# An audio tower on one core: first weight's transfer issued by ScalarE, VectorE's thresholds and floors moved, fewer spare products, a first expert unit in one piece

## The reference

```
h = patches @ W.T + b                                 # embedding
# block 0: attention with quantised activations and ternary weights
xq = act_quant(layernorm(h))                          # x * 127/max|x|, rounded, back
q, k, v = act_quant(heads(bit_linear(xq, W)))         # for Wq, Wk, Wv
   # bit_linear: s = clip(mean(|W|), EPS); Wq = clip(round(W / s), -1, 1) * s
w = act_quant(softmax(q k' / sqrt(32)));  y = act_quant(w v)
h = h + act_quant(bit_linear(y, Wp))
# 16 experts, the best two of a token weighted by a softmax
scores = x @ router_w ; g = x @ gate_w[e] ; u = x @ up_w[e]
h = h + sum_e combine[e] * ((silu(g) * u) @ down_w[e])
# block 1: attention over 4 positions, then a gated FFN between two Hadamard transforms
```

## Time and profile before

| | |
|---|---|
| median of 3 runs | 281.83 us (281.79 to 283.18) |
| profiled execution | 282.39 us, its span 280.6 us |
| TensorE busy | 264.8 us, 94% |
| VectorE busy | 227.1 us, 81% |
| ScalarE busy | 149.4 us, 53% |
| all transfers | 40.43 MB |

### The profile page before, as it was taken

One profiled execution on the slowest core, in us unless ns is written; L12 is line 12 of the kernel. 1 busy time (PEld: TensorE's weight loads), 2 busy tenths in 40 slices (PEclk: granted clock), 3 DMA queues, 4 the chain that ended last, 5 costly groups with the idle time before them and its releaser, 6 DMA issues. The chain is left out here.

```text
span 280.6 us, 3960 instructions
## 1 busy us (share of the span) xinstructions
PE 264.8 (94%) x1477; PEld 217.6 (78%) x1480; DVE 227.1 (81%) x409; ACT 149.4 (53%) x234; POOL 6.3 (2%) x19
## 2 busy tenths in 40 slices
PE   8779789989999999999999999999999999999993
PEld 3445454658899999989999897766689989999872
DVE  1969999897999988889898676888958894878783
ACT  2798772345563565655555524535466662653530
POOL 0200000000000000000000000000100000000000
PEclk9999999999999999999999999999999999999998
DMA  6960899904244808172630068095000000000003
GB/s 229 427 250 2 290 378 411 446 12 139 86 159 181 306 33 336 23 316 74 262 110 6 0 224 374 2 363 238 0 0 2 0 2 0 0 2 0 2 2 75
DMA packets 6997, 40.43 MB, mean 144 GB/s; under 512 B 1217, under 2 KB 1473, under 8 KB 5314
## 3 DMA queue, kind: packets, MB, share of 16 engines
q1 hardware_dynamic: 6978, 40.18, 37.6%
HBM read 39.13 MB, written 0.52 MB: 141 GB/s over the span
## 5 line engine op out<-in xcount | busy, mean ns | idle before, releaser
L1101 PE MATMUL bank<-s_xf_hi,s_f_hi 128*128 128x256 f32 x128 | 31.2, 282 | 0.5 <-ACT s_xf_hi L675 0.5
L1101 PE MATMUL bank<-s_xf_hi,s_f_lo 128*128 128x256 f32 x128 | 31.1, 281 | 0.0
L543 ACT ACTIVATE s_silu<-bank 128x192 f32<-128x192 f32 x32 | 10.5, 331 | 36.6 <-PE bank L883 32.6
L883 PE MATMUL bank<-s_w_hi,s_xt_hi 128*128 128x384 f32 (+1 forms) x128 | 29.3, 350 | 0.6 <-DVE s_h L1417 0.6
L883 PE MATMUL bank<-s_w_lo,s_xt_hi 128*128 128x384 f32 (+1 forms) x128 | 27.9, 339 | 0.3 <-DVE s_w_lo L1431 0.3
L883 PE MATMUL bank<-s_w_hi,s_xt_lo 128*128 128x384 f32 (+1 forms) x128 | 27.7, 338 | 0.3 <-DVE s_xt_lo L1194 0.3
L1101 PEld LDWEIGHTS bank<-s_xf_hi,s_f_hi 128*128 128x128 f32 x128 | 24.1, 188 | 1.1 <-issue 0.7
L1625 DVE TENSOR_TENSOR s_f_lo<-s_ffn_raw,s_f_hi 128x1024 fp32r<-128x1024 f32 x16 | 19.6, 1225 | 6.0 <-ACT s_f_hi L622 5.9
L1101 PEld LDWEIGHTS bank<-s_xf_hi,s_f_lo 128*128 128x128 f32 x128 | 24.1, 188 | 0.4
L883 PEld LDWEIGHTS bank<-s_w_hi,s_xt_hi 128*128 128x128 f32 x128 | 21.9, 188 | 2.2 <-DVE s_h L1417 0.8
L883 PEld LDWEIGHTS bank<-s_w_lo,s_xt_hi 128*128 128x128 f32 x128 | 22.8, 188 | 0.7 <-DVE s_w_lo L1431 0.7
(11 more groups left out here) (235 smaller groups left out, 559.7 us busy)
## 6 DMA issues: line engine op xcount, KB each, us to landing
s_moe_raw<-moe_gu SPq DMA_DIRECT2D x16, 768.0 KB, 7.2
s_ffn_raw<-ffn_w SPq DMA_DIRECT2D x4, 2048.0 KB, 10.9
s_moe_raw<-moe_dn SPq DMA_DIRECT2D x8, 768.0 KB, 4.4
s_big_raw<-att_w SPq DMA_DIRECT2D x4, 1024.0 KB, 8.9
s_big_raw<-down_w SPq DMA_DIRECT2D x4, 1024.0 KB, 8.0
s_l_raw<-l_w SPq DMA_DIRECT2D x1, 2560.0 KB, 21.1
out<-s_h SPq DMA_DIRECT2D x4, 128.0 KB, 2.3
s_tok_w<-tok_w SPq DMA_DIRECT2D x1, 256.0 KB, 2.6
```

The costliest lines, as they stand in the source:

```text
L543: act.activation(B["silu"][i % 2][:], unit_bank(i)[:, 0:F], ACT.Silu).then_inc(silu_done, 1)
L883: ins = pe.matmul(unit_bank(i)[:, 0:n], xt(k, t)[part % 2], w[:, k, 0:n], start=(first and k == 0), stop=(last and k == KC - 1))
L1101: pe.matmul(tb(j, n)[:, 0:TOK], M[w][j][:, k, n * P:(n + 1) * P], M["xf_hi"][:, k, :], start=(w == "w_hi" and k == 0), stop=False)
```

## The change

It has four parts: ScalarE and no longer SyncE issues the transfer of `att_w[0]`; in the projections' stretch the small VectorE steps stand elsewhere, the query's score factor is computed by ScalarE, and the spare products between projections are gone (12 instead of 18 before the value sums); the low part of expert 0's rest is computed while tile 0 is mixed, and that of expert 1's main part before tile 1's low input; unit 0 is computed in one piece, and unit 2 is split around unit 1.

```
-        WARM, GAP, FILL = (18, 24), 20, 7
+        WARM, GAP, FILL = (12, 24), 20, 7
 @block.sync
-            for m in range(4):
+            for m in range(1, 4):
                 if m == 2:
                     sp.dma_start(con[:], consts[:, 0:K_REP]).then_inc(ld_con, 16)
                 sp.dma_start(big_raw[:, m * KC * C:(m + 1) * KC * C], att_w[m]).then_inc(ld_att[m], 16)
 @block.scalar
+            act.dma_start(big_raw[:, 0:KC * C], att_w[0]).then_inc(ld_att[0], 16)
             act.wait_ge(bias_done, 1)
...
             main_high(1)
+            act.wait_ge(g_ready, 1)
+            act.activation(A["sh"][:, 5], A["g3"][:, 0], ACT.Copy, scale=float(D) ** -0.5).then_inc(gx_ready, 1)
             act.wait_ge(g_ready, 3)
 @block.tensor
             project(0, 0, 1)
+            weight_total(2, bank[3][:, 0:1])
             project(0, 1, 1)
-            weight_total(2, bank[3][:, 0:1])
-            early_warm(6, bank[1])
             for n in range(2):
                 for t in range(TILES):
                     project(1, n, t)
-                early_warm(6, bank[1])
             pe.wait_ge(half_ready, 3)
             for n in range(2):
                 for t in range(TILES):
                     project(2, n, t)
-                early_warm(6, bank[1])
...
+            pe.wait_ge(gu_ready, 1)
             unit_products(0, 0, True, False)
-            keep_warm(bank[5], 4)
+            unit_products(0, 2, False, False)
             pe.wait_ge(xt_ready, 3)
-            unit_products(0, 1, False, False)
+            unit_products(0, 1, False, True)
             pe.wait_ge(su_ready, 1)
             transposes(3, B["xn"], 1)
-            pe.wait_ge(gu_ready, 1)
-            unit_products(0, 2, False, True)
+            pe.wait_ge(guh_ready, 2)
+            pe.wait_ge(resth_ready, 2)
+            pe.wait_ge(turned, TURNS_FIRST)
+            unit_products(2, 0, True, False)
             pe.wait_ge(xt_hi_ready, 4)
             unit_products(1, 0, True, False)
             unit_products(1, 2, False, False)
             pe.wait_ge(xt_ready, 4)
             unit_products(1, 1, False, True)
-            pe.wait_ge(turned, TURNS_FIRST)
-            unit(2)
+            unit_products(2, 1, False, False)
+            pe.wait_ge(gu_ready, 2)
+            unit_products(2, 2, False, True)
             unit(3)
 @block.vector
+            floors(0)
             transposed_out(1)
             largest(0, 0)
-            floors(0)
+            floors(1)
+            weight_scale(2, bank[3][:, 0:1])
             largest(0, 1)
             head_factors(0)
             head_round(0, q16_ready)
-            weight_scale(2, bank[3][:, 0:1])
             head_steps(0)
-            floors(1)
             floors(2)
-            dve.wait_ge(g_ready, 1)
-            o.mark(dve.tensor_scalar(sh[:, 5], g3[:, 0], float(D) ** -0.5, None, ALU.mult))
...
-            weight_scale(3, bank[5][:, 0:1])
...
             key_products(1, A["swapped"][0])
+            weight_scale(3, bank[5][:, 0:1])
...
                 if t == 0:
+                    rest_low(0)
                     xt_low(1)
...
-            rest_low(0)
+            main_low(1)
             xt_low(3)
-            main_low(1)
             rest_low(1)
```

More of the change, by code:

```diff
@@ L1396, in _, with main_low, rest_low @@
                                   ).then_inc(xn_ready, 1)
+            def main_low(e):
+                dve.wait_ge(guh_ready, e + 1)
+                dve.tensor_tensor(main_part("w_lo", e), main_of(e), main_part("w_hi", e).bitcast(F32), ALU.subtract)
+            def rest_low(e):
+                dve.wait_ge(resth_ready, e + 1)
+                for (to, raw), (high, _) in zip(rest_parts("w_lo", e), rest_parts("w_hi", e)):
+                    last = dve.tensor_tensor(to, raw, high.bitcast(F32), ALU.subtract)
+                last.then_inc(gu_ready, 1)
             half_sw, part_sw = A["swp"][:, 0:1], A["swp"][:, 1:2]
@@ L1422, in _ @@
             normalised(1, 1, B["xn"]).then_inc(xn_ready, 1)
-            def main_low(e):
-                dve.wait_ge(guh_ready, e + 1)
-                dve.tensor_tensor(main_part("w_lo", e), main_of(e), main_part("w_hi", e).bitcast(F32), ALU.subtract)
-            def rest_low(e):
-                dve.wait_ge(resth_ready, e + 1)
-                for (to, raw), (high, _) in zip(rest_parts("w_lo", e), rest_parts("w_hi", e)):
-                    last = dve.tensor_tensor(to, raw, high.bitcast(F32), ALU.subtract)
-                last.then_inc(gu_ready, 1)
             def dn_low(p):
```

11 lines of the change are left out of this document (6 added, 5 removed).

## The result

The changed kernel takes 283.36 us (median of 20 executions, 282.17 to 284.94), the kernel before 281.85 (20 executions, 281.57 to 284.36). The ratio is 1.0045 with a 95% interval of 1.0031 to 1.006: 0.45% slower, where 0.5% faster was forecast with a range of 279.4 to 281.3. The profiled execution took 283.27 us with a span of 281.3, against 282.39 and 280.6. So one execution against the other shows 0.9 us, the medians 1.5: the profiled one of before was slower than its median by 0.5.

The account below looks back on a forecast made before the run. TensorE, busy 94%, was taken as the bound, behind a start where TensorE, VectorE and ScalarE take turns. Gains of 1.07 (order), 0.38 (queue) and 0 (expert units) made 1.45 us: 280.4 from a 281.83 median, range 279.4 to 281.3.

Parts of the forecast that it names:

- Part 1: Projections' stretch: moved thresholds and floors, score factor on ScalarE, fewer spare products; value sums start 1.07 us earlier.
- the bounds: Limits on the reordering's gain in the projections' stretch: 0.8 us (the key's gain alone) to 1.3 us.
- the second key and value swaps and the down weight's parts are issued earlier by the key's gain and keep their lead: Transfers ahead of the value sums: issued earlier by the key's gain, 0.79 us, and still in time.
- Part 2: First attention weight issued from ScalarE's queue at the start: adds 0.37 to 0.38 us of gain.
- I take d = 1.0: Delay d of the embedding, from patches and token weight sharing engines with the megabyte: 1.0 us.
- d = 1.25: Upper bound on the embedding's delay: the megabyte goes first, small data end at 5.6, 0.45 us are spare.
- The rival on this mechanism: Second queue crowds out the embedding's transfers: delay 1.25 us or more, gain 0.5 to 1.2, 280.6 to 281.3; 20%.
- Nothing, as long as the clock holds: Twelve warm products instead of eighteen before the value sums: they end well before the first value product, no cost.
- The rival had 8%: Slower: TensorE's clock falls without spare products; five value sums at half clock cost 3.0 us, 284.8; 8%.
- other gaps of a microsecond before 42 us cost nothing: Argument that TensorE's 1.1 us standstill before the value sums would not lower the clock.
- little to do from about 29.7 to 33 us: TensorE's thin stretch without the spare products, followed by a 1.1 us standstill before the sums.
- Part 3: First expert units rearranged: nothing gained, 0.7 us of TensorE's work becomes a wait before unit 4; bounds -0.1 and +0.3.

Follow-up runs that it names:

- after_fill: Changed kernel with 24 instead of 12 spare products behind the fourth total and 12 behind the swapped scales; 281.93 us, 0.9995 of the kernel before.
- fill_hold: Changed kernel, SyncE issuing `att_w[0]`, TensorE's gap filled, SyncE waiting for the down weight's first part before the experts' weights; 281.65 us, 0.9966 of before.
- after_warm: Changed kernel with 24 spare products between the projections and all 18 before the sums back; 284.43 us, 1.0052 of the kernel before.
- order_sp_warm: Changed kernel with SyncE issuing `att_w[0]` and spare products back (24 between projections, 18 before the sums); 281.77 us, 0.999 of the kernel before.
- queue_only: Kernel before with `att_w[0]` issued by ScalarE and nothing else changed; 283.46 us, ratio 1.0044.
- queue_tiny: Kernel before with only the 8 KB table `rev` issued by ScalarE instead of SyncE; 282.57 us, ratio 1.0027.
- queue_late: New order, gap filled, down weight's third part behind the value's swaps; ScalarE issues `att_w[0]` once the patches landed; 286.25 us, 1.0149 of before.

## Why the prediction was wrong

**Part 1, the order: the mechanism right, the size nearly.** 1.07 us were forecast for VectorE and, unreduced, for the sums. VectorE gained 1.21, within the bounds, in seven of the nine profiles that have the order without spare products between the projections; in the other two, `after_fill` and `fill_hold`, the clock fell between 14 and 20 us. The 1.09 measured at the sums with SyncE's issue agree with 1.07 by luck: 1.21 and an earlier landing of 0.37, less 0.49 on TensorE's queue. One step in it was wrong: "the second key and value swaps and the down weight's parts are issued earlier by the key's gain and keep their lead". The down weight's first part landed 6.0 to 6.3 us after its issue in the new order, not 5.1, and the value's swap late enough for a wait of 0.39 to 0.49 us before the second product. The first product starts the sums, which hid the second of these; the first lengthened the gap on TensorE.

**Part 2, the second queue: right mechanism, wrong size.** The step that failed is "I take d = 1.0", with d = 1.25 as its upper bound: d was 2.09. That bound let the megabyte go first and then gave the small transfers the 1.4 us that their bytes take alone. The rows show the patches used at 5.92, after the sum of the whole megabyte had begun at 5.59, and the token weight at 6.70. And a quarter of the megabyte costs 1.34 us, though its bytes need 0.6 at 413 GB/s: bytes ahead in line are not the only term. The bytes moved show one more. The token weight landed at 1.55 + 5.1 = 6.65 us, and up to then the engines had moved 6.65 x 260 = 1.73 MB:

```profile
0.00:6.65 6.65, 3.79 (x9) 1.21 (x9) 0.55 (x5) 2.93 (x3) 0.45 (x6) 1.00 0.73 260
```

The megabyte and the two small transfers have 1.44. The other 0.3 MB belong to transfers issued behind them, and at the 350 GB/s of 1.7 to 6.65 us they are worth 0.8 us (an estimate), what the bound lacks. This is an account from one profile, which no run tests; for the quarter it gives no sum. With d = 2.09 in the prediction's own steps the first side comes at 12.15 + 1.09 = 13.24 (measured 13.36), the copy at 17.76 + 1.09 = 18.85 (18.93) and the key's second maximum at 25.1 (25.2). All of the gain at the key is spent, and 0.35 are left at the value, where VectorE had 0.44. The rival on this mechanism ended at a gain of 0.5; with d = 2.09 it would have been 0.35, 281.5 us, no change. The Trainium skill's rule, drawn on in the prediction (DMA: Bandwidth & Descriptors, "Issuing engines are not separate DMA queues"), has the sense of it, and the traces agree: the sum of the first weight starts 2.4 us earlier and the first side 0.77 later.

**"Nothing, as long as the clock holds": wrong.** The rival had 8%. Its argument against, "other gaps of a microsecond before 42 us cost nothing", compared single gaps; from 30.5 to 35.3 us there are two waits (1.74 and 2.42) with one product of 0.43 between them. The prediction's own count, "little to do from about 29.7 to 33 us", ended too early: the late down weight carried it on to 35.26. The place of the damage was named wrong as well: the clock was back before the sums, and the turns ahead of them ran at half of it. What the twelve warm products were said to cost, nothing, was TensorE's 1.37 us at the sums. Priced by the run with the gap filled, it is 1.4 us of the time. That the missing spare products did it is not shown: with most of them back the clock held in `after_warm`'s profile and fell in `order_sp_warm`'s, and it fell in `queue_only`'s with all of them. What is shown is that work in the gap ahead of the turns held it. The Trainium skill (TensorE: Matmul & The Clock Gate, "Part 1: The HAM clock gate") says that the number of slow matmuls at a kernel's start varies between runs of one kernel. The 20 executions vary too, though here the slow stretch lies in the middle: 5 have a mean clock of 0.994 and 15 one between 0.977 and 0.985.

**Part 3: right.** No gain, and 0.7 us of work became 0.68 of waiting before unit 4.

**The sum.** -1.45 us were forecast, +1.5 measured. At the sums it was +0.93, and two terms make up the difference of 2.38 to the forecast there: VectorE gained 0.44 and not 1.45, which is the second queue's doing (1.01), and TensorE's queue lost 1.37, put at nothing. With the gap filled the changed kernel stands at no change (0.9995): the order's gain, 0.4% with the same fill (0.9959), is spent on the second queue. The clock adds its 1.4 us.

**What stays open.** Why the down weight's first part lands after 5.5 to 6.6 us in the new order and after 5.0 to 5.4 in the old one; why 256 KB on the second queue already cost 1.34 of the 2.09 us; why the clock falls in one profile with spare products between the projections and holds in another; and what makes executions of one kernel differ by a microsecond at a full clock.

## What to carry to other kernels

Ask of a transfer that starts earlier what it will run beside: here a megabyte on another queue filled idle bandwidth and delayed by 2.1 us the work that needed the first 0.39 MB. Before spare products go, add up TensorE's work around the place, with all its waits; where it is thin, put spare products into the waits and not between products that others need. And a wait that something occupied hid landings that were just in time: look them up again when the order changes. When single profiles are compared, measure from an event behind the first transfers: their landing alone moved by up to 1 us between executions.

## What was not expected of the hardware

- What a transfer that ScalarE issued 0.4 us earlier does to two small ones on SyncE's queue: they land 0.2 to 0.3 us later beside 8 KB, 1.8 to 2.1 beside 256 KB, 2.5 to 2.8 beside 1 MB. Their consumer starts 0.01, 1.34 and 2.09 later.
- A megabyte issued on the second queue at 3.18 us, while SyncE issued three more between 2.0 and 4.0, was used at 12.9.
- The granted clock reads 1.00 up to 33 us, 0.57 from there to 34, 0.50 from 34 to 39 and 1.00 from 40 on, around a stretch of 4.8 us in which TensorE had 0.64 us of work. From 13 to 20 us it read 0.76 in the profiled executions of `after_fill`, `fill_hold` and `queue_tiny` and 0.58 in that of `queue_late`.
